# First expert stage: the gathers and weight copies wait for VectorE's and ScalarE's semaphores instead of TensorE's

## What is computed

```python
x = x + 0.5 * _L0_ffn_ref(_layernorm(x), router_W, router_b, W1, b1, W2, b2)
x = x + _L0_attn_ref(_layernorm(x), ln1_g, ln1_b, wq, wk, wv, wo, ln2_g, ln2_b, w1, w2)
x = x + 0.5 * _L0_ffn_ref(_layernorm(x), router_W, router_b, W1, b1, W2, b2)
```

```python
logits = einsum('bsd,de->bse', x, router_W) + router_b
gates  = one_hot(argmax(softmax(logits))) * softmax(logits)
h = relu(einsum('bsd,edf->besf', x, W1) + b1)      # 128 -> 512
y = einsum('besf,efd->besd', h, W2) + b2           # 512 -> 128
out = einsum('bse,besd->bsd', gates, y)
```

## Time and profile before

| What | Value |
|---|---|
| median of 3 runs | 206.65 us (206.63 to 206.75) |
| profiled execution: span, first to last instruction | 213.1 us |
| profiled execution: own time | only the span is given |
| TensorE: busy, mean granted clock | 188.7 us (89%), 0.963 |
| VectorE, ScalarE, GpSimd busy | 121.3, 111.6, 122.0 us |
| first expert stage on TensorE, first turn to last down | 26.84 to 82.86 us |
| second expert stage, a stretch of 40 us (165 to 205) | TensorE busy 39.36 us |

### The profile page before, as it was taken

One profiled execution on the slowest core, in us unless ns is written; L12 is line 12 of the kernel. 1 busy time (PEld: TensorE's weight loads), 2 busy tenths in 40 slices (PEclk: granted clock), 3 DMA queues, 4 the chain that ended last, 5 costly groups with the idle time before them and its releaser, 6 DMA issues.

```text
span 213.1 us, 4561 instructions
## 1 busy us (share of the span) xinstructions
PE 188.7 (89%) x1410; PEld 159.3 (75%) x1410; DVE 121.3 (57%) x516; ACT 111.6 (52%) x328; POOL 122.0 (57%) x186
## 2 busy tenths in 40 slices
PE   4978599997999598898999999998996899999992
PEld 2953269986989597666876588698643899999991
DVE  4858312212212348789897946757531677777762
ACT  2666026644437455778869875131300666666670
POOL 6887456695555526834399704557673154455544
PEclk9976969999999969999999999999999999999998
DMA  5999679764778336169996000001018749676700
GB/s 191 242 381 342 208 249 342 256 197 134 243 174 286 81 85 178 41 259 415 418 410 250 0 2 3 27 28 43 27 63 285 257 165 306 206 264 223 248 27 0
DMA packets 26680, 40.26 MB, mean 189 GB/s; under 512 B 4229, under 2 KB 16296, under 8 KB 25632
## 3 DMA queue, kind: packets, MB, share of 16 engines
q1 hardware_dynamic: 21136, 33.01, 43.9%
q0 software_dynamic: 2496, 4.76, 8.3%
q10 hardware_dynamic: 3024, 2.20, 3.3%
HBM read 10.78 MB, written 14.46 MB: 118 GB/s over the span
## 4 chain that ended last, share of the span: by engine, by line
PE 63%; DVE 13%; issue 9%; POOL 6%; DMA 4%; ACT 2%; another core or an unknown queue 1%; POOLq 0%; DVEq 0%
PE bank L1102 20%; PE bank L1119 18%; PE bank L1238 6%; PE bank L1254 5%; DMA xn_scratch<-xn 3%; PE bank L1095 3%; PE bank L928 2%; DVE stat L1323 2%; POOL xn L581 1%; PE bank L1193 1%; PE bank L1179 1%; DMA Xg<-xn_scratch,srcu 1%; PE bank L1203 1%; DVE x L1558 1%; PE bank L1210 1%
## 5 line engine op out<-in xcount | busy, mean ns | idle before, releaser
L747 ACT ACTIVATE hT<-bank,ewc_own 128x128 f32<-128x128 f32 x184 | 51.6, 373 | 56.7 <-PE bank L1102 38.2
L1102 PE MATMUL bank<-xT,ewc_own 128*128 128x128 f32 x368 | 51.1, 284 | 6.5 <-DVE xT L1455 3.8
L1102 PEld LDWEIGHTS bank<-xT,ewc_own 128*128 128x128 f32 x368 | 46.3, 198 | 9.2 <-issue 9.2
L1119 PE MATMUL bank<-ew,hT 128*128 x368 | 49.4, 278 | 0.0
L1119 PEld LDWEIGHTS bank<-ew,hT 128*128 128x128 f32 x368 | 45.5, 195 | 0.2 <-issue 0.2
L681 POOL DMA_INDIRECT out_dram<-ysb,eqrq x23 | 22.6, 982 | 26.6 <-issue 17.6
L609 POOL DMA_INDIRECT Xg<-xn_scratch,srcu x23 | 22.0, 958 | 15.0 <-PE bank L1102 4.8
L1461 DVE TENSOR_TENSOR ysb<-bank,ewc_own 128x128 f32<-128x128 f32 x23 | 6.7, 289 | 34.1 <-PE bank L1119 26.5
L634 POOL DMA_INDIRECT xnT<-slot_scratch,posu x16 | 15.8, 987 | 13.5 <-DVE ysb L1461 4.3
L928 PE MATMUL bank<-ones_bf 128*128 128x512 bf16 x66 | 19.9, 428 | 3.1 <-POOL ident L499 2.7
L673 POOL DMA_INDIRECT row_scratch<-pay,posu x16 | 15.8, 987 | 10.8 <-DVE posu L1428 6.8
(11 more groups left out here) (239 smaller groups left out, 303.7 us busy)
## 6 DMA issues: line engine op xcount, KB each, us to landing
ewc_own<-ew SPq DMA_DIRECT2D x46, 322.0 KB
row_scratch<-xn SPq DMA_DIRECT2D x8, 1024.0 KB, 10.6
ew<-in_L_ffn_W_dram SPq DMA_DIRECT2D x1, 2048.0 KB, 11.1
slot_scratch<-ysb SPq DMA_DIRECT2D x23, 64.0 KB
ew<-in_L_ffn_W_dram SPq DMA_DIRECT2D x5, 256.0 KB, 9.4
eqrq<-row_scratch SPq DMA_DIRECT2D x18, 70.0 KB
x<-in_L_attn_x_dram SPq DMA_DIRECT2D x4, 256.0 KB, 3.6
xn_scratch<-xn ACTq DMA_DIRECT2D x4, 256.0 KB, 6.2
```

Source lines behind the costliest of these rows:

```text
L747: last = A(hT[:, t.slot, c * P:(c + 1) * P], up_bank(k, c)[:, c * P:(c + 1) * P], ACT.Relu, scale=0.5 if m else 1.0, bias=ewc[t.ahead][:, ...
L1102: last = mm(up_bank(k, c)[:, c * P:(c + 1) * P], ewc[t.ahead][:, c * P:(c + 1) * P], xT[:, t.slot, :], start=True, stop=True)
L1119: last = mm(bank[4 + t.parity][:, 0:D], hT[:, t.slot, c * P:(c + 1) * P], ew[:, bass.ds(e[k], 1), W2_AT + c * D:W2_AT + (c + 1) * D].squee ...
```

## The change

Three waits name another semaphore; the counts stay. SP's pace before a weight copy waits for xT_ready (DVE) instead of xg_T (PE). POOL's pace waits for xT_ready instead of xg_T, and in the second halves for hT_ready (ACT) instead of h_ps (PE). No instruction is added, left out or moved on any engine. The second expert stage keeps its wait on xg_T.

```diff
@@ -428,7 +428,7 @@
                 if k == 1:
                     sp.wait_ge(g_in[0], 16)
                 if k >= FIRST:
-                    sp.wait_ge(xg_T, max(1, k - LEAD))
+                    sp.wait_ge(xT_ready, max(1, k - LEAD))
                 if k >= UNROLL:
                     sp.wait_ge(y_ready, 1 + k - UNROLL)
                     store_slots(k - UNROLL)
@@ -599,9 +599,9 @@
             def paced(n):
 
                 half = max(0, int(STEP * n)) - 1
-                pool.wait_ge(xg_T, GT + half // 2)
+                pool.wait_ge(xT_ready, GT + half // 2)
                 if half % 2:
-                    pool.wait_ge(h_ps, GT - 1 + half // 2)
+                    pool.wait_ge(hT_ready, GT - 1 + half // 2)
```

## The result

The change makes the kernel slower: 208.75 us (median of 16 runs, 207.37 to 210.6) against 206.5 us for the kernel before, measured beside it (16 runs, 204.72 to 208.59). The ratio is 1.0109 with a 95% interval of 1.0085 to 1.0134, that is +2.25 us (1.8 to 2.8), where +0.6 us was forecast and 208.0 was the upper end of the range. All ratios here come with their intervals from the fast runs alone and are not quotients of the medians beside them, from which they differ by up to 0.2%. The profiled execution of the changed kernel has an own time of 207.82 us, 0.9 us under the median of its runs, and a span of 206.1 us.

What follows compares the result with a forecast made beforehand. TensorE, busy for 89% of the span, was taken to bound the kernel, so its waits in the first expert stage cost time. Terms 0 + 0.6 + 0 + 0 gave +0.6 us, 207.2 us; range 202.6 to 208.0.

Steps and rivals of the forecast that it cites:

- SP's weight copies: SP's queue: copies 8 to 11 go out 0.2 us later, hidden by a distance of 9.6 us; sum 0.
- Gather 5 starts 1.18 us later: POOL's first paced gather waits for ScalarE to finish tile 1, then 0.75 us: start moves from 32.47 to 33.65.
- So I take the middle, 3.41: Gather 5's time to tile 5's turn, put between 4.00 and 2.82 us: turn at 37.06, 0.6 us later.
- the end of 1.18: Upper end at tile 5's turn: if gather 5 again takes 4.00 us, TensorE loses the whole 1.18 us.
- The other gathers, 0 with a bound of 0.7: Gathers after 5: gather 6 stays covered, gather 9 about 1.2 us later with about 3.3 us left; cost 0, up to 0.7.
- The bring_backs, 0: First group's last bring_back moves 1.18 us later, hidden behind result 17: cost 0, with 1.0 us for the range.
- the rival with the late tail: First group's bring_back lands behind result 17, up to 1.0 us on top of up to 1.2: 207.6 to 208.8; chance 0.05.
- The cure by prompt semaphores, 0.30: First expert stage: POOL's waits make TensorE's semaphores late; the change frees 4.6 us: 202.6, or 201.1 with the clock; chance 0.30.
- The last sign that the prediction named: If the profile loses the lateness and the runs are not faster, the lateness belonged to the profile.
- The delay is hidden, 0.20: At tile 5, the gather takes 2.8 us without profiling, so TensorE's wait stays: 206.5 to 206.9 us; chance 0.20.

Runs made afterwards that it cites:

- the first experiment: Only SP's weight-copy wait moved to VectorE's xT_ready, POOL's pace as before, against the kernel before: 206.06 us, ratio 0.9981.
- the first profile of before: Unchanged kernel before, the profiled execution shown ahead of the prediction: span 213.1 us, where the runs take 206.65 us.
- the second profile of before: Unchanged kernel before, run and profiled once more: 206.77 us, ratio 1.0003, span 204.8 us.
- ScalarE's half: Only POOL's second halves wait for ScalarE's hT_ready instead of h_ps, against the kernel before: 207.73 us, ratio 1.0065.
- the second and third trial on the tail: Whole change with gathers 18 to 22 and bring_backs on TensorE's semaphores, ratio 1.0113; whole change with bring_backs on them, memsets cut to one column, 1.0055.
- the first trial on the tail: Whole change, but all gathers on TensorE's semaphores again, only the bring_backs of the first two groups on the new ones: 206.61 us, ratio 1.0015.
- both gathers earlier: Kernel before, with gather 5 unpaced and gather 9 waiting for no more than gather 8 does: 206.02 us, ratio 0.9958.
- VectorE's half: Whole change, but POOL's second halves on TensorE's h_ps; SP and POOL's whole tiles wait for VectorE's xT_ready: 206.75 us, ratio 1.0006.

## Why the prediction was wrong

The sign and the mechanism were right, the size was not: +0.6 us forecast, +2.25 measured. The step that failed is the price of a late gather: 3.41 us for gather 5, and full cover for gather 9. Both took about 4 us, more than the time that they had until their turns. By the prediction's steps:

- **SP's weight copies, 0.** Right: SP's change alone gives 0.9981.
- **Gather 5 starts 1.18 us later, by ScalarE's tile 1 plus 0.75.** Right: 6.42 us behind turn 0 against 5.18 in the first experiment, 1.24 later.
- **"So I take the middle, 3.41": +0.6 at the turn of tile 5.** This is the term that was mis-sized. The gather took 37.44 - 33.24 = 4.20 us to the turn, not 3.41, and turn 5 came 10.62 us behind turn 0 against 9.51: +1.1. The nearest row, the same gather's 4.00 us, stood there and gave the end of 1.18; averaging it with gather 0's 2.82, from another place of the stage, was the mistake. The reason given for the middle does not hold either: 0.75 is the mean DMA share of ten us, but over the gather's own time, 33.24 to 37.44, the share in the changed kernel is 0.90, hardly less than the 0.95 of the same gather before (32.47 to 36.47). Gather 0 went at 0.26.
- **The other gathers, 0 with a bound of 0.7.** Gather 9 starts at 40.60, where the prediction had 40.6; that is luck, since it was counted from the late start of the first profile of before. Behind turn 0 it starts 13.78 us against 11.49, 2.3 us later and not 1.2, as it waits for tile 4, whose up stands behind the late turn 5. Its transfer then took 44.59 - 40.60 = 3.99 us, again the long end, where the prediction had 3.3 us of cover: turn 9 waits, and from turn 5 to turn 9 pass 7.15 us against 6.75, +0.4. With gather 5 alone put right, 1.0033 is left; with gather 9 too, 0.9998.
- **The bring_backs, 0, and the rival with the late tail.** In the profile the last bring_back took 68.92 - 64.81 = 4.11 us to the take_back, the long end once more where the short one was taken, and VectorE waits 1.02 us, the bound that the prediction had. From turn 22 to the first matmul of the attention block (L1179) the changed kernel takes 8.82 us and the first experiment 8.16, 0.66 more. The sum 1.1 + 0.4 + 0.66 comes near the measured 2.25, but only its first two terms are shown. Against the second profile of before the same places give 1.29 us up to turn 9 and 0.49 in the tail. And the runs do not bear the third term out. The six kernels in which gathers 5 and 9 are both late (the whole change, POOL's waits, the bring_backs restored, ScalarE's half, the second and third trial on the tail) have ratios of 1.0051 to 1.0113. The six in which neither is late have 0.9958 to 1.0015. Yet three of these six (the first trial on the tail, gathers 5 and 9 restored, both gathers earlier) have the wait ahead of the take_back at its full 1.2 to 1.4 us. The rival with the late tail, 207.6 to 208.8, holds the measured 208.75 and was given 0.05; that it does is luck as far as its tail goes.
- **The cure by prompt semaphores, 0.30.** Wrong. The evidence against it was in the prediction: the profiled execution was 6.5 us longer than the runs, and its lateness explained just that. The last sign that the prediction named came true: the profile of the changed kernel has lost the lateness (0.04 us at result 17), and the runs are not faster. The second profile of before, with the old waits, shows 0.03 us. No time was there to be won, and the low end of the range, 202.6, rested on it alone.
- **The delay is hidden, 0.20.** Wrong by the first term: nothing covers gather 5.

What stays open is the tail. VectorE's wait ahead of the first take_back is nothing in the first profile of before and with SP's change alone, under 0.1 us with VectorE's half and 0.45 in the second profile of before; it is 1.0 to 1.5 us in the ten other profiles. That does not follow when the bring_backs go out (3.97 us ahead of result 17 with and without the wait), nor how early POOL's queue is, and the version with gathers 5 and 9 restored carries a wait of 1.33 us at no loss in its time. Which transfers they meet there was not tried. The DMA records of the traces hold one hint. A transfer of GpSimd's ends in sixteen packets of 4 bytes, and one 16 KB packet of the queue called "instruction" falls into this stretch in each profile. In the eleven profiles with a wait of 0.45 us or more, this packet starts 0.26 us or more ahead of the fifteenth of the sixteen, and the last of them ends 0.38 to 1.43 us behind the fifteenth; in the three others the packet starts at most 0.09 us ahead of it, and the last follows within 0.07 us. That the packet holds the transfer up is argued from this and not shown.

## What to carry to other kernels

Before a profile's waits are given a cause, hold its span against the times of the runs: a wait that makes up just the difference may belong to that execution alone, and then no change can win it; a second profile tells. A transfer that is issued later in a stretch where it already arrives with no slack passes the whole delay on: price it with the same transfer's own row, not with a faster one from elsewhere, and take the DMA share over its own time, not over a round stretch. And look for the few waits at the head of a queue: here two of 26 carried the loss, and moving those two the other way won time, while the delay that the queue handed on behind them cost nothing up to the last gather.

## What was not expected of the hardware

In one profiled execution TensorE's results were seen up to 3.6 us late, for most of a stage at full granted clock. In the thirteen other profiles, a second one of the same kernel among them, every result up to 65 us is taken within 0.04 us of its down's end. And a gather of 128 rows did not take less at a middling DMA share than at a high one: from its start to the turn that waited for it 4.00 us at a share of 0.95 over that time (gather 5 before), 4.20 us at 0.90 and 3.99 us at 0.52 (gathers 5 and 9 of the changed kernel); gather 0 took 2.82 us at 0.26.
